# Perceiver layer on one core: constants in one transfer, first key chunks on other items, context pieces ahead of exponentials

## What is computed

```
x = layernorm(x);  ln = LN(x) * ln_w + ln_b
q, qx, k, v   = fp8_linear(ln, wq | wqx | wk | wv)      # rounded to an fp8 grid, scale per column
core          = softmax(LN(q) LN(k)^T / sqrt(128)) v    # own tokens, 64 keys, 8 groups x 2 heads
kx, vx        = split(ctx @ w_kv_x^T)                   # ctx: (8, 1601, 512)
xout          = softmax(LN(qx) LN(kx)^T / sqrt(128)) vx # 1601 keys, 8 groups x 2 heads
x             = x + quant([core, xout]) @ wproj^T * scale
```

## Time and profile before

| | us |
|---|---|
| median of 3 runs | 1973.66 (1973.33 to 1975.82) |
| profiled execution, its own time | 1969.9 |
| its span, first to last instruction | 1968.6 |
| TensorE matmuls busy | 1885.5 (96%) |
| VectorE busy | 1116.8 (57%) |
| ScalarE busy | 955.4 (49%) |
| GpSimd busy | 627.1 (32%) |
| mean granted TensorE clock | 0.986 |
| chain that ended last, TensorE's share | 83% |

### The profile page before, as it was taken

One profiled execution on the slowest core, in us unless ns is written; L12 is line 12 of the kernel. 1 busy time (PEld: TensorE's weight loads), 2 busy tenths in 40 slices (PEclk: granted clock), 3 DMA queues, 4 the chain that ended last, 5 costly groups with the idle time before them and its releaser, 6 DMA issues.

```text
span 1968.6 us, 30916 instructions
## 1 busy us (share of the span) xinstructions
PE 1885.5 (96%) x10129; PEld 1600.8 (81%) x10129; DVE 1116.8 (57%) x2969; ACT 955.4 (49%) x1956; POOL 627.1 (32%) x742
## 2 busy tenths in 40 slices
PE   6889999999999999999999999999999999999879
PEld 4778888888888888888888888888888888876357
DVE  6765565545564556456655665566556654446853
ACT  5654454545564555445544554455445544435711
POOL 4325543322232223233333333333333332301010
PEclk9999999999999999999999999999999999999969
DMA  7674354534544354335443544354435432465020
GB/s 250 224 255 150 112 157 126 161 112 125 165 149 143 112 175 135 109 115 170 138 146 112 172 152 140 112 178 152 140 112 178 152 113 80 152 230 184 4 86 22
DMA packets 220496, 280.67 MB, mean 143 GB/s; under 512 B 61161, under 2 KB 123882, under 8 KB 220338
## 3 DMA queue, kind: packets, MB, share of 16 engines
q1 hardware_dynamic: 209410, 277.73, 44.9%
q10 hardware_dynamic: 8880, 0.54, 0.3%
q0 software_dynamic: 2048, 0.43, 0.1%
HBM read 238.85 MB, written 39.22 MB: 141 GB/s over the span
## 4 chain that ended last, share of the span: by engine, by line
PE 83%; DVE 6%; ACT 5%; DMA 3%; issue 2%; ACTq 0%; SPq 0%; POOL 0%; DVEq 0%; POOLq 0%
PE kx_ps L510 9%; PE u_ps L616 9%; PE kx_ps L512 9%; PE kx_ps L514 9%; PE u_ps L617 9%; PE u_ps L618 9%; PE t_ps L601 5%; PE sc_ps L587 3%; PE ssq_ps L529 2%; PE sc_ps L588 2%; PE sc_ps L589 2%; PE t_ps L642 2%; DMA stage<-in_ctx_n 2%; PE t_ps L625 1%; ACT prob L1204 1%
## 5 line engine op out<-in xcount | busy, mean ns | idle before, releaser
L510 PE MATMUL kx_ps<-ctxT_hi,wk_hi 128*128 128x400 f32 (+1 forms) x1024 | 364.8, 356 | 10.5 <-DVE ctxT_lo L292 10.5
L512 PE MATMUL kx_ps<-ctxT_lo,wk_hi 128*128 128x400 f32 (+1 forms) x1024 | 355.0, 347 | 0.0
L514 PE MATMUL kx_ps<-ctxT_hi,wk_lo 128*128 128x400 f32 (+1 forms) x1024 | 354.8, 347 | 0.0
L616 PE MATMUL u_ps<-ctxN_hi,pt_hi 128*128 128x512 f32 (+1 forms) x832 | 341.1, 410 | 7.6 <-DVE pt_lo L838 7.6
L617 PE MATMUL u_ps<-ctxN_lo,pt_hi 128*128 128x512 f32 (+1 forms) x832 | 330.2, 397 | 0.0
L618 PE MATMUL u_ps<-ctxN_hi,pt_lo 128*128 128x512 f32 (+1 forms) x832 | 328.8, 395 | 0.0
L838 DVE TENSOR_TENSOR pt_lo<-t_ps,pt_hi 128x512 fp32r<-128x512 f32 (+1 forms) x256 | 144.5, 586 | 248.7 <-ACT pt_hi L1086 248.7
L1055 ACT ACTIVATE kx_hi<-kx_ps 128x400 fp32r<-128x400 f32 (+1 forms) x256 | 128.9, 504 | 312.5 <-PE kx_ps L514 310.3
L1086 ACT ACTIVATE pt_hi<-t_ps 128x512 fp32r<-128x512 f32 (+1 forms) x256 | 125.5, 522 | 262.5 <-PE t_ps L601 262.4
L765 DVE TENSOR_TENSOR kx_lo<-kx_ps,kx_hi 128x400 fp32r<-128x400 f32 (+1 forms) x256 | 146.7, 573 | 179.1 <-ACT sq L1057 178.6
L820 DVE CUSTOM_DVE_ANT_0 prob<-sc_ps,rstd_bc 128x400 f32<-128x400 f32 (+2 forms) x256 | 136.4, 570 | 140.5 <-PE sc_ps L589 140.5
(11 more groups left out here) (282 smaller groups left out, 3495.5 us busy)
## 6 DMA issues: line engine op xcount, KB each, us to landing
rstd_bc<-scratch_rstd SPq DMA_DIRECT2D x64, 804.0 KB, 6.0
stage<-in_ctx_t SPq DMA_DIRECT2D x96, 267.0 KB, 4.3
stage<-in_ctx_n SPq DMA_DIRECT2D x96, 256.0 KB, 6.1
wk_hi<-scratch_wk_s SPq DMA_DIRECT2D x56, 256.0 KB, 3.0
wk_lo<-scratch_wk_s SPq DMA_DIRECT2D x56, 256.0 KB, 3.3
wv_hi<-scratch_wv_s SPq DMA_DIRECT2D x56, 256.0 KB, 4.8
wv_lo<-scratch_wv_s SPq DMA_DIRECT2D x56, 256.0 KB, 5.6
scratch_own_rows<-out_sb SPq DMA_DIRECT2D x32, 256.0 KB, 3.7
```

The source lines that it names most:

```text
L510: PE.matmul(kx_ps[:, j % 2, 0:w], wk_hi[:, g % 2, i, :], ctxT_hi[:, i, c0:c0 + w], start=(i == 0), stop=False)
L512: PE.matmul(kx_ps[:, j % 2, 0:w], wk_hi[:, g % 2, i, :], ctxT_lo[:, i, c0:c0 + w], start=False, stop=False)
L514: mm = PE.matmul(kx_ps[:, j % 2, 0:w], wk_lo[:, g % 2, i, :], ctxT_hi[:, i, c0:c0 + w], start=False, stop=(i == C - 1))
L616: PE.matmul(u_ps[:], pt_hi[0:w, t % 2, cols], ctxN_hi[0:w, y, :], start=(y == 0), stop=False)
```

## The change

The columns, the small rows and the identity become one tile `consts` and one transfer; GpSimd doesn't wait for it any more, VectorE waits for it after the input statistics. The first key chunks go to other items, with pieces and squares; on VectorE `weights_low` stands ahead of `keys_low`. In round -1 the pieces of place 0 go to places 3 and 6, and VectorE waits for the stored outputs after the softmax bias. In rounds 5, 13, ... the four pieces 8 to 11 all stand at place 3. `load_wv_halves(8)` goes behind the refills of round 7. TensorE waits for the threshold after the first of the two turns.

```diff
-        self.cols = self.sb(stack, "cols", [P, N_COLS])
-        self.rows = self.sb(stack, "rows", [P, N_ROWS - LATE])
-        self.ident = self.sb(stack, "ident", [P, P])
+        self.consts = self.sb(stack, "consts", [P, N_COLS + N_ROWS - LATE + P])
+        self.cols, self.rows = self.consts[:, 0:N_COLS], self.consts[:, N_COLS:N_COLS + N_ROWS - LATE]
+        self.ident = self.consts[:, N_COLS + N_ROWS - LATE:]
...
-        self.ACT.dma_start(self.cols[:], self.dram["cols"]).then_inc(self.const_in, 16)
-        self.ACT.dma_start(self.rows[:], self.dram["rows"][0, LATE:N_ROWS].partition_broadcast(P)).then_inc(self.const_in, 16)
-        self.ACT.dma_start(self.ident[:], self.dram["ident"]).then_inc(self.const_in, 16)
+        self.ACT.dma_start(self.consts[:], self.dram["consts"]).then_inc(self.const_in, 16)
...
-        for eng in (self.PE, self.DVE, self.ACT, self.POOL):
-            eng.wait_ge(self.const_in, 48)
+        for eng in (self.PE, self.ACT):
+            eng.wait_ge(self.const_in, 16)
...
             if n == -1:
-                whose, at, left = 0, {0: 2, 3: 2, 5: 2, 7: 1}, range(PIECES - 7, PIECES)
+                whose, at, left = 0, {3: 2, 5: 2, 6: 2, 7: 1}, range(PIECES - 7, PIECES)
...
             elif not final and g == G_ - 3:
-                at, left = {0: 2, 1: 2, 3: 2, 4: 2}, range(C, T0)
+                at, left = {0: 2, 1: 2, 3: 4}, range(C, T0)
...
-        first_high = {0: range(0, 5), 6: range(5, 7), 7: range(7, 8), 9: range(8, 10), 10: range(10, 11), 11: range(11, 12)}
-        first_low = {3: range(0, 2), 4: range(2, 3), 6: range(3, 5), 7: range(5, 7), 8: range(7, 8), 10: range(8, 10),
-                     11: range(10, 12)}
-        first_keys = {8 + 2 * j: (0, j) for j in range(4)} | {18 + 2 * j: (1, j) for j in range(4)}
+        first_high = {0: range(0, 5), 6: range(5, 7), 7: range(7, 8), 9: range(8, 10), 12: range(10, 12)}
+        first_low = {2: range(0, 1), 3: range(1, 3), 6: range(3, 5), 7: range(5, 7), 8: range(7, 8), 10: range(8, 10),
+                     14: range(10, 12)}
+        first_keys = {8: (0, 0), 11: (0, 1), 15: (0, 2), 17: (0, 3), 20: (1, 0), 22: (1, 1), 24: (1, 2), 26: (1, 3)}
...
-                PE.wait_ge(t_thr_set, 2)
...
-                if i == 17:
+                if i == 19:
                     key_squares(0)
...
                 if s:
                     turn_prob(n + 1, 0)
+                if n == MAKES - 1:
+                    PE.wait_ge(t_thr_set, 2)
+                if s:
                     turn_prob(n + 1, 1)
...
+            for t in range(4):
+                V.wait_ge(x_in[t], 16)
+                norm.vector_stats(t, x_sb)
+            V.wait_ge(core.const_in, 16)
             a = COLS["q_in"][0]
             V.reciprocal(recip[:], core.cols[:, a:a + 16]).then_inc(scales_set, 1)
...
-            for t in range(4):
-                V.wait_ge(x_in[t], 16)
-                norm.vector_stats(t, x_sb)
...
-                if i - 1 in first_keys:
-                    keys_low(*first_keys[i - 1])
                 if n + 1 < NB:
                     after(V, product_done, 4 * n)
                     for c in ((0,), (1, 2, 3), (), ())[t]:
                         weights_low(n + 1, c)
+                if i - 1 in first_keys:
+                    keys_low(*first_keys[i - 1])
...
-            for t in range(4):
-                V.wait_ge(out_stored[t], stored_before(NB))
             V.reciprocal(recip_o, recip_o).then_inc(set_up, 1)
...
                     softmax_bias(n + 1)
+                if n == -1:
+                    for t in range(4):
+                        V.wait_ge(out_stored[t], stored_before(NB))
...
-                if i == 18:
+                if i == 20:
                     squares_out(0)
...
-                if i == 22:
+                if i == 24:
                     key_rstd(0)
...
-                if i == 24:
+                if i == 26:
                     load_rstd(0)
...
-                if n + 1 >= G_ and n + 1 < N:
+                if n >= G_ and n + 1 < N:
                     load_wv_halves(n + 1)
...
                 refill(5, 6, 7)
+                if n + 1 == G_:
+                    load_wv_halves(n + 1)
```

More of the change, by code:

```diff
@@ L2283 @@
         "ctx_n": ctx,
-        "cols": np.concatenate([column(parts[n]) for n in COLS], axis=1),
-        "rows": np.concatenate([row_parts[n].reshape(-1) for n in ROWS]).reshape(1, N_ROWS),
-        "ident": np.eye(P, dtype=np.float32),
+        "consts": np.concatenate([column(parts[n]) for n in COLS] + [np.tile(row_parts[n].reshape(1, -1), (P, 1)) for n in ROWS
+                                 if ROWS[n][0] >= LATE] + [np.eye(P, dtype=np.float32)], axis=1),
+        "rows": np.concatenate([row_parts[n].reshape(-1) for n in ROWS if ROWS[n][1] <= LATE]).reshape(1, LATE),
         "rankmat": ((lane[:, None] // 64 == lane[None, :] // 64) * (lane[:, None] <= lane[None, :])
```

## The result

The changed kernel takes 1954.33 us (median of 5 runs, 1953.60 to 1957.32) against 1973.33 us in the runs beside it: ratio 0.9906, 95% interval 0.9893 to 0.9920.

What follows compares the result with a forecast made beforehand. TensorE, busy 1885.5 of 1968.6 us, was taken as the bound, leaving 83 us of standstill plus clock loss. 2.8 + 1.0 + 0 + 5.5 + 4.5 + 0.5 = 14.3 off 1973.66 gave 1959.4 us, range 1951 to 1967.

Steps and rivals of the forecast that it cites:

- A: Start: one constants transfer, statistics first, small products free of the memset; gain 2.8 us (1.5 to 3.4).
- the floor of the weight block: Start: ScalarE's weight halves begin when the first block lands at 10.98, capping the gain at 3.4 us.
- The shift is kept: Start: a VectorE and ScalarE chain to the first product, DMA queues empty, so the earlier start is not lost.
- B: First key chunks: stop stays, about 4.4 us, only later; gain 1.0 us (-1.5 to 6.9).
- my reading: Start: port rule frees one-input products beside a memset unless in 2-port mode; then A 1.4, total 12.9.
- C: Round -1: removed stop's 2.4 us eaten by a new one, loads behind the broadcast; gain 0 (+2.4 to -3.0).
- rival 2: Both new stops bite harder, C = -3 and B = -1: gain 9.3, 1964.4 us; chance 0.17.
- D: Seven batch boundaries: four pieces at place 3 remove the 0.85 us stops; gain 5.5 us (4 to 6).
- The slower rival: Seven boundaries: a late piece 11 makes the four pieces hold the exponential; 1989.4 us; chance 0.04.
- E: Weight halves behind the pieces in round 7: 3.19 us stop and clock loss go; gain 4.5 us (3.2 to 4.6).
- F: Threshold: first turn goes ahead of the 1.69 us wait; gain 0.5 us (0 to 0.6).
- most of the idle time: Whole kernel: about 30 us of TensorE's idle time lies in the tail after 1780 us, left alone.

Runs made afterwards that it cites:

- run 7: Changed kernel with GpSimd's memset held until the input statistics are done, so it runs beside VectorE's small products; 1960.66 us (one execution).
- run 6: Changed kernel with the constants in three transfers again, statistics still ahead of them; 1957.18 us (one execution).
- run 1: Changed kernel with the first key chunks, their pieces and the order on VectorE put back as before; 1957.05 us, ratio 0.9915.
- run 2: Changed kernel with first-stage chunks and pieces at their old places, new VectorE order (weight halves ahead of key halves) kept; 1953.58 us, ratio 0.9902.
- run 3: Changed kernel with key chunks (0,2), (0,3) and those of group 1 two items later, pieces unmoved; 1952.36 us (one execution).
- run 4: Changed kernel with round -1's pieces at places 0, 3, 5, 7 as before, the wait for stored outputs still moved; 1952.5 us (one execution).
- run 9: Changed kernel with the edits of run 4 and run 5 together; 1948.1 us, ratio 0.9870.
- run 10: Changed kernel with the edits of run 4, run 5 and run 3 together; 1946.71 us, ratio 0.9867.
- run 8: Changed kernel with D, E and F undone; 1969.83 us, ratio 0.9987.
- run 5: Changed kernel with the weight halves loaded behind the refills of round 7 in every batch, not only the first; 1951.06 us, ratio 0.9883.

## Why the prediction was right, point by point

**A (2.8, 1.5 to 3.4): mis-sized.** The mechanisms were right: statistics first, and the small products freed of the memset (run 7). The first product moved by 4.6 us, beyond the end of the range. The failing term was the landing of the tiles: I took the fourth near 8.2, from landings of 2.9 to 6.1 us, and the floor of the weight block at 10.98, as if neither depended on the constants. They do: with three transfers back, both came later (run 6: the fourth statistics at 8.70 against 6.51, ScalarE's weight halves at 11.35 against 9.53). "The shift is kept" was wrong too: in run 1, without B, the first product is 4.05 us earlier than before and `key_squares(1)` 3.25 (inside the range), with the weight wait grown from 0.93 to 2.21 us on the way. Nor were the DMA queues empty there: the DMA share from 12 to 23 us is 0.45 in the kernel before.

By the Trainium skill (SBUF — State Buffer, section "SBUF: two separate sides") a VectorE instruction in a 2-port mode, or one with two SBUF inputs against a GpSimd op that reads, excludes GpSimd from the shared ports, the one that starts first holding them. Under my reading, in which a one-input product beside a memset is free, run 7 should have shown 0.54 us; it showed 1.49. Whether the products ran in a 2-port mode, which would save the rule, no run here shows.

**B (1.0, -1.5 to 6.9): right.** The stop came where it was expected: it ended at 61.46, where 64.0 less A's 2.8 makes 61.2. It was 5.59 instead of about 4.4 us long, as TensorE got there at 55.9 instead of 56.8, the start having moved further than A allowed. B is 0.2 to 2.2 us by `key_squares(1)` (run 1). But it is the order of two calls on VectorE that earns it (run 2); moving the chunks as the change does only moved the stop. The forecast took it for granted that a later chunk gains nothing more; run 3 shows that two items further the stage is 1.8 to 3.7 us shorter.

**C (0, -3.0 to 2.4): right in kind.** The old stop went, the new one came with the cause named, loads 23 and 24 behind the broadcast. The broadcast went out at 148.71, where the forecast has 152.8 less the shift of 3.9 that A and B had made by then. The gain is 0.6 us in this profile where 0 was expected: ScalarE had piece 23 at 154.90, the forecast at 159.4 less 3.9, so 155.5. Runs 4, 9 and 10 are the proof of the cause: with these loads ahead of the broadcast none has the stop, while all eight profiles with the loads behind it do, 1.54 to 3.30 us long.

The 0.6 us are luck of this one profile. From `key_squares(1)` to `(3)`, the clock behind the stop with it, the kernel before takes 43.2 us, the eight profiles with the changed round -1 take 42.5 to 45.8 (44.2 in the mean), and runs 4, 9 and 10 take 41.2 to 41.3. Against the one profile of before, C as built is between +0.7 and -2.6, -1.0 in the mean; five of the eight lose 1.2 to 2.6 us, in the direction of rival 2. The moved wait without the moved pieces gives 2.0.

The rule quoted from the Trainium skill (DMA: Bandwidth & Descriptors, section "Queues, rings and completion order") that a ring is consumed in order agrees with this: the piece behind the broadcast took 5.8 us, one without it 3.7; no run here separates the order in the ring from shared bandwidth.

**D (5.5, 4 to 6): mis-sized by a little.** Seven steps of 1.1, 1.1, 1.1, 0.7, 0.8, 0.8 and 0.8 us in the ladder make 6.5, and undoing them costs 6.7 (run 8). The sum counted the stops, 0.85 or less each; the first three gave 0.25 more than the stop. It isn't the clock, which was granted at 1.00 around the first boundary before and after (290 to 306 and 296 to 310 us). TensorE's idle time there falls by 0.85 and its busy time by 0.24; why the latter falls at three boundaries of seven stays open. The slower rival did not come: no exponential was held by the four pieces.

**E (4.5, 3.2 to 4.6): right.** 4.52 us in the ladder, 3.19 of stop and the rest clock. Undoing it costs 5.4 (run 8), with a stop of 3.87 us instead of 3.19, so one pair of profiles doesn't fix the size. The forecast looked only at the first boundary; the change leaves the weight halves ahead of the pieces at the later ones, and run 5 found 4.3 us there.

**F (0.5, 0 to 0.6): right** by run 8, 0.5 us. The pair of profiles has 2.0 us at this place. Run 8 has the old stop of 1.69 us and is still 1.5 us quicker there than the kernel before, in whose profile the clock had fallen as well: from 811 to 815 us it was granted at 0.57, in run 8 at 1.00. These 1.5 us are the profile's and not the change's.

**The sum.** 3.9 for A and B, 0.6 for C, 6.5 for D, 4.5 for E, 2.0 at F make 17.6 of the ladder; 1.8 go at small stops, mostly one of 1.35 us at the second boundary, which run 5 removes, and then 0.7 in the tail: 15.1 of span, where 14.3 were forecast. D, E and F don't make that stop: run 8, with the three undone, has it too (1.37 us). In the kernel before the same piece, behind the same weight halves, landed in 6.2 us instead of the 8.1 of run 8, and nothing stopped. So some of the agreement is luck: 1.5 us of clock at F and this stop, neither of them forecast, nearly cancel.

The clock that E and F give back was lost elsewhere, and TensorE's busy time is the same: the clock granted from 60 to 68 us is 0.79 before and 0.65 after, and that of 8 us at the end of the ladder 0.79 (from 1708) and 0.57 (from 1690). The forecast's "most of the idle time" in the tail is 29.3 of 83 us.

Of the 5.1 us by which the median lies under the forecast value, 0.8 are these, 0.3 that the median before, over five runs, is 1973.33, and 3.9 that the profiled executions stood differently to their medians. The profiles can't say more of these 3.9 us.

## What to carry to other kernels

A wait named for a compute engine at a batch boundary may be for a transfer: look at what stands ahead of that transfer in its issuing queue, and put bulk transfers that nobody needs soon behind the small ones that somebody waits for. Do it at every boundary, not only at the first where it is seen. A few small-row transfers at the start cost more in what they hold up than in their own landing; joining them pays even where nobody waits for them. When an engine's queue bounds a stretch, moving the consumer moves the stop; it shortens it only where the consumer then takes things in the order in which that queue makes them. The rest needs a shorter or better ordered queue.

## What the runs showed of the hardware that was not expected

**The clock after a short stop.** Behind stops of nearly the same length, at the same place, the clock sometimes falls and sometimes doesn't. Windows of 3 us behind `key_squares(2)`, columns as above: the changed kernel (stop 1.54 us), run 3 (2.13), run 5 (1.89), run 2 (3.30).

```profile
157.27:160.27 3.00, 3.00 (x16) 2.51 (x17) 0.97 (x2) 0.60 (x1) 2.91 (x4) 1.00 0.00 0
```

```profile
154.53:157.53 3.00, 3.00 (x16) 2.49 (x17) 0.97 (x2) 0.60 (x1) 2.83 (x5) 1.00 0.00 0
```

```profile
156.62:159.62 3.00, 3.00 (x10) 2.52 (x11) 0.97 (x2) 0.60 (x1) 2.83 (x5) 0.50 0.00 0
```

```profile
157.38:160.38 3.00, 3.00 (x10) 2.51 (x11) 2.04 (x2) 0.60 (x1) 2.82 (x4) 0.50 0.20 60
```

At 0.50, its level of 1.2 GHz, TensorE does 10 instructions instead of 16 in the window, and the ladder loses about 1.6 us. A stop of 2.13 us kept the full 2.4 GHz and one of 1.89 us did not, so the length of the stop alone doesn't decide. Of the eight profiles with a stop here the clock stayed at 1.00 behind 1.54, 1.66 and 2.13 us and fell behind 1.89, 1.97, 2.36, 3.10 and 3.30. The threshold's stop of 1.69 us says the same: behind it the clock fell in the kernel before and stayed at 1.00 in run 8. A stop of 1.5 to 2.4 us may thus cost 1.6 us more or nothing, and a range should hold both.

**Kernels with the same first stage differ in it.** The changed kernel and runs 4, 5, 8 and 9 have the same code for the first stage, and `key_squares(1)` at 138.49, 136.96, 137.52, 138.92 and 138.38. The stop at chunk (0,2) ends at 60.43 to 61.46 us in them, and behind it the clock differs (windows of the changed kernel and of run 4):

```profile
58.00:68.00 10.00, 6.54 (x23) 6.14 (x24) 5.91 (x11) 3.28 (x7) 0.00 (x0) 0.66 0.70 221
```

```profile
58.00:68.00 10.00, 7.57 (x30) 6.92 (x31) 6.44 (x11) 3.70 (x7) 0.00 (x0) 0.83 0.75 251
```

Differences under 2 us in this stage can't be read from one profile each, which is why run 1's 0.6 us for B is only its order of size.
